# Isomorphism round of a graph network: two batches of edge embeddings in a ring, embedded one to two batches ahead

## The chip, the cores and the metric

The kernel runs on one core of a Trainium2 chip. The metric is the device time of one execution in microseconds (us), lower is better. "Before" is the median of three runs.

## The reference

Four graph networks follow one another on 50,000 nodes of 128 features and 25,000 edges sorted by destination. After each the result is added to its input and layer-normalised. The change touches the second network, the isomorphism round:

```python
edge_emb = edge_attr @ bond_W + bond_b                    # 16 -> 128 per edge
message = gelu(x[src] + edge_emb) * edge_weight1          # exact gelu
agg = segment_sum(message, dst, num_segments=50000)
h = relu(((1 + eps) * x + agg) @ W1 + b1)                 # 128 -> 256
x = layernorm(x + h @ W2 + b2)
```

## The kernel before, in words

The kernel is written with explicit semaphores: every engine has a program of its own, order and waits are written by hand, and instructions of one engine run in program order. Eight rounds of message passing follow one another; round 3 (`k == 3`, kind GIN) is the isomorphism round.

Edges come in 196 tiles of 128, in 28 batches of 7 tiles. Nodes are taken from the top down in 98 halves of 512 nodes, two halves a step, so 49 steps of 1024 nodes. The sum over edges is a matmul of messages with one-hot columns, in two float16 parts: `msg[.., 0:D]` the high part, `msg[.., D:2D]` the low part.

What happens to one batch `e` of edges in round 3:
- GpSimd (POOL, `gin_edges`): seven indirect DMAs fetch the source rows into one of four slots of `raw` (`gather`, L696), one DMA fetches the edge attributes into the single buffer `attr_now` (`attributes`, L709), and `hand_over` waits until both have landed and counts `batch_in` up (L720).
- TensorE (PE, `embed`, L1091): attributes times bond weights, into the two PSUM banks `p_edge` and `p_tr`.
- VectorE (DVE, `embedded_sum`, L1520): rows plus embedding, into `edge_v`, in two parts.
- ScalarE (ACT, `gelu`, L801): gelu of `edge_v` in place.
- POOL (`weigh`, L726): times the edge weight, in place.
- ACT (`batch`, L807): copy to the high part of `msg`.
- DVE (`batch`, L1548): low part, the difference.

There is one `edge_v` and one `embedded` pair of banks. So in the loop over batches `batch(e)` on each engine finishes batch `e` and starts batch `e + 1`: ACT copies `e`, then does the gelu of `e + 1`; DVE makes the low part of `e`, then the sum of `e + 1`; PE embeds `e + 1`.

A step `it` of the round on each engine:
- PE: the batches that step `it + 1` needs; the one-hot matmuls (L1132, L1134) of half 1 of `it` and the residual (L1158); `hidden` of half 0 (L1196); `biased_rows` of half 1 of `it - 1` (L1204, L1208); the one-hot matmuls of half 0 of `it + 1`; `hidden` of half 1; `biased_rows` of half 0 of `it`.
- ACT: the same batches; sums out of PSUM (L847); relu of the hidden layer, half 0 (L856); square root of the variance (L882); sums out of the next half; normalise half (L897); relu, half 1 (L856); normalise the other half.
- DVE (`gin_step`): the same batches; one-hots of half 0 of `it + 1` (L1566); add the residual of half 1 (L1647) and its statistics (L1658, L1663); `scale_rows` (L1775); one-hots of half 1 of `it + 1`; reciprocal and shift for the normalisation (L1672, L1674); add and statistics of half 0.

Which batches belong to a step stands in a list in SBUF that each engine loads into its registers at the head of a step (`values_load`). The list asks for a batch in two of three steps, and for one batch before the first step. The loop over batches is a branch and a loop in registers. ACT loads a function table (`ACT_TABLE_LOAD`) where the next function is not in the loaded one, and at the head of a loop's body or behind it, where the state is not known to the program.

## Time and profile before

| | |
|---|---|
| median of 3 runs | 5383.45 us (5371.6 to 5387.2) |
| profiled execution, its own time | 5378.48 us |
| its span, from the first to the last instruction | 5376.4 us |
| busy share of the span | PE 82%, DVE 64%, ACT 45%, POOL 36% |
| the isomorphism round in the span | first gather at 1484.15 us, steady steps from 1554.5 to 2199.1 us, last batch copied at 2201.47 us |

PE is busy most of the time over the whole kernel. The rounds differ, so the change has to be read in the stretch from 1484 us on, of which the section of rows below shows the part that is used. An idle time with "<-" behind it was ended by the instruction named; "issue" is time in which the engine waited for nothing that the profile shows.

### The profile page before, as it was taken

What the parts mean: (1) busy time and instruction counts of PE and PEld (TensorE: products, weight loads), DVE (VectorE), ACT (ScalarE), POOL (GpSimd) and SP (SyncE); (2) the same over time, 40 slices, a digit from 0 to 9 for tenths busy, and PEclk for the clock granted to TensorE, in tenths of its full rate; (3) what the DMA queues carried; (4) which work ended last, traced back from release to release, by engine and by line L of the source; (5) the groups of instructions that cost most, each with busy time, mean ns of one, the idle gap of its engine ahead of it and who ended that gap; (6) DMA issues with size and microseconds to landing.
All of it is one profiled execution on the core that took longest, in us unless ns stands there. A gap on an engine that the chain in (4) does not pass through costs nothing.

```text
span 5376.4 us, 129953 instructions
## 1 busy us (share of the span) xinstructions
PE 4387.9 (82%) x25128; PEld 2875.8 (53%) x25129; DVE 3446.8 (64%) x10510; ACT 2416.5 (45%) x4969; POOL 1921.9 (36%) x1886
## 2 busy tenths in 40 slices
PE   6998997777878888867777688887799996888895
PEld 4664554433445555535554355543577773677672
DVE  5553454787545555449997688876566663777774
ACT  2442442555257777526664466664222211333332
POOL 5650782654033333016550443310433312333310
PEclk9999999899889999989999899998899999999997
DMA  4663884665234444325553466653444433443432
GB/s 142 217 210 117 260 270 149 195 192 174 90 122 147 149 146 145 111 96 171 174 172 103 145 210 205 211 173 109 137 136 137 140 116 109 129 130 125 128 100 76
DMA packets 443919, 815.61 MB, mean 152 GB/s; under 512 B 70872, under 2 KB 76818, under 8 KB 443828
## 3 DMA queue, kind: packets, MB, share of 16 engines
q1 hardware_dynamic: 389172, 697.28, 38.4%
q0 software_dynamic: 54656, 117.32, 8.9%
q8 instruction: 33, 0.54, 0.0%
q14 instruction: 58, 0.48, 0.0%
HBM read 480.10 MB, written 334.22 MB: 151 GB/s over the span
## 4 chain that ended last, share of the span: by engine, by line
PE 46%; issue 15%; DVE 14%; DVEq 8%; ACT 7%; POOL 5%; DMA 3%; ACTq 2%; SPq 1%; POOLq 0%
PE p_agg L1132 8%; PE p_edge L1119 7%; PE p_agg L1134 7%; PE p_tr L1119 6%; POOL raw L696 4%; PE p_agg L1165 4%; DVE onehot L1566 4%; DVE stats L1658 3%; ACT u L916 2%; PE p_wide L1252 2%; ACT o L897 2%; DVEq L373 2%; PE p_agg L1158 2%; DVEq L1566 2%; PE p_dense L1208 2%
## 5 line engine op out<-in xcount | busy, mean ns | idle before, releaser
L1566 DVE TENSOR_SCALAR onehot<-iota,dst_f,negbase 128x512 f16<-128x512 f16 (+1 forms) x2848 | 1126.1, 449 | 815.6 <-PE p_agg L1165 305.3
L1132 PE MATMUL p_agg<-onehot,msg 128*128 128x512 f16 (+1 forms) x2848 | 1138.3, 400 | 596.5 <-DVE onehot L1566 338.6
L696 POOL DMA_INDIRECT raw<-node_s,src_i x980 | 958.7, 978 | 1449.1 <-DMA node_s<-o 561.4
L1134 PE MATMUL p_agg<-onehot,msg 128*128 128x512 f16 (+1 forms) x2848 | 1140.3, 400 | 0.0
L1132 PEld LDWEIGHTS p_agg<-onehot,msg 128*128 x2848 | 281.8, 99 | 941.4 <-issue 791.1
L696 POOL DMA_INDIRECT raw<-node_x,src_i x392 | 378.8, 966 | 551.0 <-DMA feature<-more_masked 253.6
L897 ACT ACTIVATE o<-v_ring,nmr,rstd 128x128 f32 (+1 forms) x1176 | 472.5, 482 | 76.6 <-DVE nmr L1674 71.5
L1165 PE MATMUL p_agg<-h_in,w 128*128 128x512 f32 x784 | 443.3, 649 | 22.9 <-DMA h_in<-feature 21.9
L1658 DVE BATCH_NORM_STATS2 stats<-v_ring 128x6 f32 (+1 forms) x1960 | 417.7, 278 | 44.3 <-DVE v_ring L1647 15.9
L916 ACT ACTIVATE u<-v_ring,nmr,rstd 128x128 f32 (+1 forms) x784 | 312.5, 481 | 225.0 <-DVE res_in L1704 134.7
L1134 PEld LDWEIGHTS p_agg<-onehot,msg 128*128 x2848 | 282.7, 99 | 219.1 <-issue 32.0
L867 ACT ACTIVATE u<-p_agg,bias 128x512 f32<-128x512 f32 x196 | 134.7, 687 | 551.8 <-PE p_agg L1165 550.8
L1531 DVE SCALAR_TENSOR_TENSOR hid<-type_in,p_wide 128x512 f32<-128x512 f32 (+2 forms) x456 | 261.7, 618 | 89.9 <-PE p_wide L1110 31.7
L752 POOL COPY edge_v<-raw 128x896 f32<-128x896 f32 x56 | 52.2, 931 | 702.6 <-PE p_wide L1110 691.4
L882 ACT ACTIVATE std<-mv,eps_col 128x8 f32<-128x8 f32 x245 | 73.0, 298 | 500.5 <-DVE mv L1663 487.7
L1531 DVE SCALAR_TENSOR_TENSOR more_masked<-type_in,p_wide 128x512 f32<-128x512 f32 (+2 forms) x456 | 267.2, 619 | 39.3 <-PE p_edge L1119 39.3
L1647 DVE TENSOR_TENSOR v_ring<-p_dense,res_in 128x512 f32 (+1 forms) x196 | 135.3, 691 | 205.0 <-PE p_dense L1208 169.1
L1252 PEld LDWEIGHTS p_wide<-w,u 128*128 128x128 f32 x1568 | 205.2, 192 | 101.1 <-issue 89.5
L867 ACT ACTIVATE u<-p_agg,sage_bias 128x512 f32<-128x512 f32 x196 | 133.4, 680 | 269.0 <-PE p_agg L1165 267.3
L1158 PEld LDWEIGHTS p_agg<-hid,h_in 128*128 128x128 f32 x1568 | 224.9, 213 | 47.1 <-issue 38.9
L1158 PE MATMUL p_agg<-hid,h_in 128*128 128x128 f32 x1568 | 233.4, 297 | 0.0
L696 POOL DMA_INDIRECT raw<-in_x,src_i x196 | 194.8, 994 | 105.1 <-issue 54.2
(260 smaller groups left out, 7741.9 us busy)
## 6 DMA issues: line engine op xcount, KB each, us to landing
node_s<-o SPq DMA_DIRECT2D x392, 256.0 KB
h_in<-feature SPq DMA_DIRECT2D x392, 256.0 KB
feature<-u SPq DMA_DIRECT2D x294, 256.0 KB
node_x<-o SPq DMA_DIRECT2D x294, 256.0 KB
res_in<-node_x SPq DMA_DIRECT2D x294, 256.0 KB
h_in<-node_s SPq DMA_DIRECT2D x196, 256.0 KB
h_t<-dinv_scratch SPq DMA_DIRECT2D x196, 256.0 KB
h_in<-in_x SPq DMA_DIRECT2D x98, 256.0 KB
```

The costliest lines, as they stand in the source:

```text
L696: nc.gpsimd.indirect_dma_start(out=raw[:, (e % RING) * BATCH + j, :], out_offset=None, in_=src_d, in_offset=bass.IndirectOffsetOnAxis(ap=s ...
L897: last = nc.scalar.activation(o[:, b, :], tile_ap(v_ring, (it % 2) * BLOCKS + b), ACT.Identity, bias=nmr[0][:, b:b + 1], scale=rstd[0][:, ...
L916: last = nc.scalar.activation(u[:, b, :], tile_ap(v_ring, (it % 2) * BLOCKS + b), ACT.Identity, bias=nmr[0][:, b:b + 1], scale=rstd[0][:, ...
L1119: last = nc.tensor.matmul(related[part][:, j * D:(j + 1) * D], masked[m][:, j * P:(j + 1) * P], w[:, m, :], start=m == 0 and j == 0, stop= ...
L1132: nc.tensor.matmul(p_agg[:, a, :], tile_ap(msg, t, 0, D), oh, start=first, stop=True, skip_group_check=True)
L1134: return nc.tensor.matmul(p_agg[:, a, :], tile_ap(msg, t, D, 2 * D), oh, start=False, stop=True, skip_group_check=True)
L1158: last = nc.tensor.matmul(p_agg[:, a, b * P:(b + 1) * P], h_in[:, 4 * a + b, :], scaled_ident if k == 3 else two_ident, start=False, stop= ...
L1165: nc.tensor.matmul(p_agg[:, a, :], w[:, REL if rel else 3 if k == 1 else 5, :], half_buf(h_in, a), start=False, stop=True, skip_group_chec ...
L1252: last = nc.tensor.matmul(p_wide[:, a, b * D:(b + 1) * D], u[:, 4 * a + b, :], w[:, 2 if k == 0 else 4, :], start=True, stop=True)
L1531: V.scalar_tensor_tensor(out=masked[m][:, cols], in0=flat(type_in[:, bass.ds(e % RING, 1), j0 * P:j1 * P]), scalar=float(m), in1=p_wide[:, ...
L1566: return V.tensor_scalar(tile_ap(onehot, slot), iota[:, :], dst_f[:, bass.ds(t, 1)], negbase[:, bass.ds(it * 2 + a, 1)], ALU.subtract, ALU ...
L1658: last = V.bn_stats(stats[0][:, b, :], tile_ap(v_ring, (it % 2) * BLOCKS + b))
```

## The change

A ring of two batches of float32 edge values, `edge_ring`, takes the place of `edge_v` in this round. It lies in the memory of `type_in`, which only the last two rounds use. Each engine now works on different batches: PE embeds `e + 3`, DVE makes the low part of `e` and the sum of `e + 2`, ACT does the gelu of `e + 1` before the copy of `e`, POOL gathers `e + 4` and hands over `e + 3`.

The batches of a step move too. The list of the step after next is used (`it + 2` in place of `it + 1`). PE does them at the end of its step, behind `biased_rows(it, 0)`; DVE behind the one-hots of half 1 and before `scale_and_move`; ACT behind the relu of half 0 and before `deviation`. Before the first step PE embeds three batches and then the one of the early loop, so four in all, and POOL fetches four batches and hands three over before the first `weigh`. The attribute DMA moves into `hand_over`, behind the gathers of the next batch. The semaphores' totals follow.

```diff
@@ -79,7 +79,7 @@
 
         rows, last, gin, gcn, two = part == 0, part >= 2, part == 3, part >= 4, part == 5
         self.loaded, self.stored = pair("loaded", 16 * NPAIR), pair("put", 16 * NPAIR)
-        self.batch_in = one("taken", 0 if rel else BATCHES + gin)
+        self.batch_in = one("taken", 0 if rel else BATCHES + 3 * gin)
         self.hi_done = one("high", (1 + rel) * BATCHES)
         self.lo_done = one("low", (1 + rel) * BATCHES)
         self.every_ready = one("every", NHALF)
@@ -100,8 +100,8 @@
         self.sum_made = one("sum_made", NHALF, two)
         self.hidden_made = one("hidden_made", 2 * NHALF, gin)
         self.hidden_done = one("hidden_done", 2 * NHALF, gin)
-        self.emb_done = one("emb_done", 2 * BATCHES + 2, gin)
-        self.emb_used = one("emb_used", 2 * BATCHES + 4, gin)
+        self.emb_done = one("emb_done", 2 * (BATCHES + 3), gin)
+        self.emb_used = one("emb_used", 2 * (BATCHES + 2) + 2, gin)
         self.gelu_done = one("gelu_done", BATCHES + 1, gin)
         self.weighed = one("weighed_edges", BATCHES + 1, gin)
         self.res_loaded = pair("residual", 16 * NPAIR, last and part != 4)
@@ -178,6 +178,7 @@
         ew = sb("ew", [P, TILES])
         ew1 = sb("ew1", [P, TILES])
         type_in = sb("type_in", [P, RING, BATCH * P], F16)
+        edge_ring = flat(type_in[:, :, :]).bitcast(F32).rearrange("p (j d) -> p j d", d=D)
         ecol = sb("ecol", [P, TILES, 4], F16)
 
         onehot = sb("onehot", [P, 2 * EVERY + MORE * GROUP, HALF], F16)
@@ -705,16 +706,20 @@
                 all_stored(pool, r - 1)
 
                 def attributes(e):
-                    wait(pool, q.emb_done, 2 * e)
-                    pool.dma_start(attr_now[0:BATCH * DE, :], A["edge_attr_16"][e:e + 1, :, :].rearrange("o f e -> f (o e)")
-                                   ).then_inc(gathered[e % RING], 16)
+                    if 0 < e < BATCHES:
+                        wait(pool, q.emb_done, 2 * e)
+                        pool.dma_start(attr_now[0:BATCH * DE, :],
+                                       A["edge_attr_16"][e:e + 1, :, :].rearrange("o f e -> f (o e)")
+                                       ).then_inc(gathered[e % RING], 16)
 
                 def gather(e):
-                    if e >= RING:
-                        wait(pool, q.emb_used, 2 * (e - RING + 1) + 2)
-                    gather_batch(r, src_d, e)
+                    if e < BATCHES:
+                        if e >= RING:
+                            wait(pool, q.emb_used, 2 * (e - RING + 1) + 2)
+                        gather_batch(r, src_d, e)
 
                 def hand_over(e):
+                    attributes(e)
                     if e < BATCHES:
                         pool.wait_ge(gathered[e % RING], 16 * (per_batch[r] * (e // RING + 1) + landed_before[r]))
                     pool.sem_inc(q.batch_in.semaphore, 1)
@@ -722,21 +727,19 @@
                 def weigh(e):
                     wait(pool, q.gelu_done, e + 1)
                     at = min(e, BATCHES - 1) * BATCH
+                    mine = edge_ring[:, (e % 2) * BATCH:(e % 2 + 1) * BATCH, :]
                     share = ew1[:, at:at + BATCH].unsqueeze(2).to_broadcast([P, BATCH, D])
-                    nc.gpsimd.tensor_tensor(edge_v[:, :, :], edge_v[:, :, :], share, ALU.mult
-                                            ).then_inc(q.weighed.semaphore, 1)
-
-                gather(0)
-                hand_over(0)
-                gather(1)
+                    nc.gpsimd.tensor_tensor(mine, mine, share, ALU.mult).then_inc(q.weighed.semaphore, 1)
+
+                for e in range(3):
+                    gather(e)
+                    hand_over(e)
+                gather(3)
                 for e in range(BATCHES + 1):
                     weigh(e)
-                    if e + 1 < BATCHES:
-                        attributes(e + 1)
-                    if e + 2 < BATCHES:
-                        gather(e + 2)
+                    gather(e + 4)
                     if e < BATCHES:
-                        hand_over(e + 1)
+                        hand_over(e + 3)
 
             def sage(r, src_d, rel, weight):
                 q = S[r]
@@ -796,17 +799,19 @@
             def sage(r, k, rel):
                 q = S[r]
 
+                def edge_slot(e):
+                    return edge_ring[:, bass.ds((e % 2) * BATCH, BATCH), :]
+
                 def gelu(e):
                     wait_apart(act, q.emb_used, 2 * e + 4)
-                    nc.scalar.activation(flat(edge_v[:, :, :]), flat(edge_v[:, :, :]), ACT.Gelu
-                                         ).then_inc(q.gelu_done.semaphore, 1)
+                    nc.scalar.activation(edge_slot(e), edge_slot(e), ACT.Gelu).then_inc(q.gelu_done.semaphore, 1)
 
                 def batch(e):
                     if k == 3:
+                        gelu(e + 1)
                         wait_apart(act, q.weighed, e + 1)
-                        nc.scalar.activation(msg[:, bass.ds(e * BATCH, BATCH), 0:D], edge_v[:, :, :], ACT.Copy
+                        nc.scalar.activation(msg[:, bass.ds(e * BATCH, BATCH), 0:D], edge_slot(e), ACT.Copy
                                              ).then_inc(q.hi_done.semaphore, 1)
-                        gelu(e + 1)
                         return
                     if not rel:
                         wait_apart(act, q.batch_in, e + 1)
@@ -822,7 +827,7 @@
                                          raw[:, bass.ds((e % RING) * BATCH, BATCH), :], ACT.Copy).then_inc(q.hi_done.semaphore, 1)
 
                 def batches(it):
-                    if rel or k == 3:
+                    if rel:
                         if exists(it + 1):
                             each_batch(act, *batch_list(act, PT, it + 1), batch)
                         return
@@ -956,7 +961,8 @@
                     last.then_inc(q.normed2.semaphore, 1)
 
                 def step(it):
-                    batches(it)
+                    if k != 3:
+                        batches(it)
                     if k == 4:
                         relu_out(it - 1, 1)
                         scale_rows(it - 3)
@@ -989,6 +995,7 @@
                     elif k == 3:
                         sums_out(it, 1)
                         hidden(it, 0)
+                        batches(it)
                         deviation(it - 1)
                         sums_out(it + 1, 0)
                         normalise(it - 1, (0,))
@@ -1094,7 +1101,7 @@
 
                 def batch(e):
                     if k == 3:
-                        embed(e + 1)
+                        embed(e + 3)
                         return
                     for part in range(2):
                         wait_apart(pe, q.lo_done, e * 2 + (part - 1))
@@ -1256,10 +1263,9 @@
                     last.then_inc(q.rows_done.semaphore, 1)
 
                 def step(it):
+                    these = ()
                     if exists(it + 1):
-                        if k == 3:
-                            these, (now, after) = odd_list(pe, PT, it * 2 + 1)
-                        elif rel:
+                        if rel or (k == 3 and exists(it + 2)):
                             (e0, e1, e2), (now, after) = later_list(pe, PT, it * 2 + 1)
                             these = e1, e2
                         else:
@@ -1267,17 +1273,22 @@
                     elif exists(it):
                         now = single_list(pe, PT, it * 2 + 1)
                     if k == 3:
-                        if exists(it + 1):
-                            each_batch(pe, *these, batch)
+                        if is_zero(it):
+                            each_batch(pe, e0, e1, batch)
                         if exists(it):
                             first_half(it, 1, now)
                         hidden(it, 0)
                         biased_rows(it - 1, 1)
                         if exists(it + 1):
-                            wait_apart(pe, q.lo_done, these[1])
+                            if these:
+                                wait_apart(pe, q.lo_done, e1)
+                            else:
+                                wait(pe, q.lo_done, BATCHES)
                             first_half(it + 1, 0, after)
                         hidden(it, 1)
                         biased_rows(it, 0)
+                        if these:
+                            each_batch(pe, *these, batch)
                         return
                     if k >= 4:
                         if exists(it):
@@ -1317,7 +1328,8 @@
                         turn_edges(0, part)
                 if k == 3:
                     pe.wait_ge(bond_in, 16 * len(bond_weights))
-                    embed(0)
+                    for e in range(3):
+                        embed(e)
                 end = early_batches(pe, PT, batch if rel or k == 3 else None)
                 wait_apart(pe, q.lo_done, end * (1 + rel))
                 first_half(0, 0, single_list(pe, PT, 0))
@@ -1513,12 +1525,15 @@
             def sage_round(r, k, rel):
                 q, rounds_s = S[r], R[r]
 
+                def edge_slot(e, j0=0, j1=BATCH):
+                    return edge_ring[:, bass.ds((e % 2) * BATCH + j0, j1 - j0), :]
+
                 def embedded_sum(e):
                     wait_apart(dve, q.batch_in, e + 1)
                     for part, (j0, j1) in enumerate(QUARTERS):
                         wait_apart(dve, q.emb_done, 2 * e + (part + 1))
                         V.tensor_tensor(
-                            edge_v[:, j0:j1, :], raw[:, bass.ds((e % RING) * BATCH + j0, j1 - j0), :],
+                            edge_slot(e, j0, j1), raw[:, bass.ds((e % RING) * BATCH + j0, j1 - j0), :],
                             embedded[part][:, 0:(j1 - j0) * D].rearrange("p (j d) -> p j d", d=D), ALU.add
                             ).then_inc(q.emb_used.semaphore, 1)
 
@@ -1545,11 +1560,11 @@
                 def batch(e):
                     if k == 3:
                         wait_apart(dve, q.hi_done, e + 1)
-                        V.tensor_tensor(msg[:, bass.ds(e * BATCH, BATCH), D:2 * D], edge_v[:, :, :],
+                        V.tensor_tensor(msg[:, bass.ds(e * BATCH, BATCH), D:2 * D], edge_slot(e),
                                         msg[:, bass.ds(e * BATCH, BATCH), 0:D], ALU.subtract
                                         ).then_inc(q.lo_done.semaphore, 1)
                         wait_apart(dve, q.lo_done, e + 1)
-                        embedded_sum(e + 1)
+                        embedded_sum(e + 2)
                         return
                     if rel:
                         masks(e, 1)
@@ -1592,10 +1607,9 @@
                         if exists(it):
                             more_onehots(it, 1, single_list(dve, PT, it * 2 + 1))
                         return None, None, None
-                    if rel or k == 3:
+                    if rel:
                         these, (now, after) = odd_list(dve, PT, it * 2 + 1)
-                        if rel:
-                            first_onehots(it + 1, 0, after[0])
+                        first_onehots(it + 1, 0, after[0])
                         each_batch(dve, *these, batch)
                         ahead = None
                     elif exists(it + 2):
@@ -1785,6 +1799,7 @@
                     scale_rows(it - 2)
                     if now:
                         first_onehots(it + 1, 1, after)
+                    batches_ahead(ahead)
                     scale_and_move(it - 1)
                     add(it, 0)
                     statistics(it, 0)
@@ -1840,6 +1855,7 @@
                 first_onehots(0, 1, after[0])
                 if k == 3:
                     embedded_sum(0)
+                    embedded_sum(1)
                 if rel:
                     masks(0, 0)
                 early_batches(dve, PT, batch)
```

## Rows read from the trace of the kernel before

**Rows 1.** The page's chain that ended last: shares of the span by engine.
```profile
PE 46%; issue 15%; DVE 14%; DVEq 8%; ACT 7%; POOL 5%; DMA 3%; ACTq 2%; SPq 1%; POOLq 0%
```

**Rows 2.** Windows of the round: from:to, length; busy us (instructions) of PE, PEld, DVE, ACT, POOL; granted clock; DMA share; GB/s.
```profile
1484.00:1511.00 27.00, 7.30 (x12) 3.16 (x13) 10.41 (x29) 3.18 (x3) 19.62 (x20) 0.50 0.25 69
...
1554.50:2199.10 644.60, 547.44 (x2847) 343.31 (x2848) 353.53 (x1139) 481.15 (x767) 214.74 (x213) 1.00 0.45 146
...
2199.10:2330.00 130.90, 99.90 (x468) 59.18 (x466) 55.75 (x182) 57.64 (x97) 1.77 (x1) 0.91 0.27 90
```

**Rows 3.** Waits, 1554.5 to 2199.1 us: who waited for whom: total us, times, longest.
```profile
PE p_agg L1132 <- DVE onehot L1566: 47.8, 25, 2.4
...
PE p_wide L1196 <- ACT hid L856: 20.3, 23, 0.9
...
DVE msg L1548 <- ACT msg L807: 97.1, 25, 4.4
```

**Rows 4.** Timeline of a step with a batch: start, us, engine, line, operation [idle before].
```profile
1658.16 1.28 ACT L801 ACT_TABLE_LOAD   x1 [3.44 <-DVE edge_v L1520]
...
1659.46 0.95 ACT L801 ACTIVATE edge_v<-edge_v 128x896 f32<-128x896 f32 x1
...
1659.71 0.39 PE L1132 MATMUL p_agg<-onehot,msg 128*128 128x512 f16 x1 [1.89 <-DVE onehot L1566]
...
1660.49 1.68 POOL L726 TENSOR_TENSOR edge_v<-edge_v,ew 128x896 f32<-128x896 f32 x1 [6.68 <-ACT edge_v L801]
...
1661.61 1.65 DVE L1775 TENSOR_TENSOR u<-o,dinv 128x1024 f32<-128x1024 f32 x1
```

**Rows 5.** Timeline of a step without a batch (from 1568.35) and its neighbours.
```profile
1565.14 2.05 PE L1208 MATMUL p_dense<-w,hid 128*128 128x128 f32 x16
...
1568.35 0.39 PE L1132 MATMUL p_agg<-onehot,msg 128*128 128x512 f16 x1 [1.15 <-issue]
...
1572.73 2.05 PE L1208 MATMUL p_dense<-w,hid 128*128 128x128 f32 x16
...
1572.78 1.26 ACT L856 ACTIVATE hid<-p_wide,b_col 128x512 f32<-128x512 f32 x2
...
1577.57 1.23 DVE L1775 TENSOR_TENSOR u<-o,dinv 128x1024 f32<-128x1024 f32 x1
...
1578.72 1.05 DVE L1566 TENSOR_SCALAR onehot<-iota,dst_f,negbase 128x512 f16<-128x512 f16 x3
...
1578.93 2.05 PE L1208 MATMUL p_dense<-w,hid 128*128 128x128 f32 x16
...
1581.91 1.10 PE L1091 MATMUL p_edge<-bond,attr_now 113*128 113x512 f32 x2 [0.93 <-issue]
...
1583.48 0.38 PE L1132 MATMUL p_agg<-onehot,msg 128*128 128x512 f16 x1
...
1587.49 1.09 DVE L1548 TENSOR_TENSOR msg<-edge_v,msg 128x896 f32 x1 [4.41 <-ACT msg L807]
...
1589.91 0.55 DVE L1520 TENSOR_TENSOR edge_v<-raw,p_tr 128x384 f32<-128x384 f32 x1
```

**Rows 6.** Timeline of the start of the round.
```profile
1495.35 0.95 POOL L696 DMA_INDIRECT raw<-node_x,src_i  x1 [2.31 <-DMA raw<-node_x,src_i]
...
1503.84 1.69 POOL L726 TENSOR_TENSOR edge_v<-edge_v,ew 128x896 f32<-128x896 f32 x1
...
1505.46 0.60 POOL L709 DMA_DIRECT2D attr_now<-in_edge_attr  x1
...
1508.11 2.05 PE L1091 MATMUL p_edge<-bond,attr_now 113*128 113x512 f32 x2 [9.95 <-POOLq L720]
```

**Rows 7.** Timeline of PE: first matmul of the steps 42, 43 and 44.
```profile
2199.10 0.38 PE L1132 MATMUL p_agg<-onehot,msg 128*128 128x512 f16 x1
...
2224.02 0.39 PE L1132 MATMUL p_agg<-onehot,msg 128*128 128x512 f16 x1 [1.04 <-issue]
...
2244.53 0.39 PE L1132 MATMUL p_agg<-onehot,msg 128*128 128x512 f16 x1 [1.00 <-issue]
```

## The prediction

> **What bounds the kernel now.** I read the page's chain first: PE has the largest share of it, 46%, and DVE and PE's own issue come next [rows 1]. That is a mean over eight rounds, so I went on to windows of the one round that the change touches. It falls into three parts [rows 2]: a start of 27 us in which PE does next to nothing and its granted clock is 0.50, the lower of its two levels (1.2 GHz); a steady stretch of 644.6 us at a clock of 1.00 (2.4 GHz), in which PE is busy 547 us; and an end without batches. The steady stretch holds the 39 steps from step 3 to step 41. The reader should see there that PE is the bound, but not all the time.
>
> The view of waits says what PE waits for [rows 3]. In 25 steps, those with a batch, it waits 1.9 us for one-hots (47.8 us in all) and in nearly all of them 0.9 us for ACT's relu (20.3 us). Nothing else of size is there. Together that is 68.1 us, and it is what the change can win at most in the stretch. The timeline of such a step shows why [rows 4]: ACT's copy comes late, DVE waits for it (97.1 us in all, [rows 3]), makes low part and sum, and only then starts its one-hots, with which PE starts again; ACT meanwhile waits 3.4 us for the sum before the gelu. The batch stands at the head of the step, in front of everything.
>
> **The change, part by part.** I count a step from its first one-hot matmul, "A". In the step of [rows 5] A is at 1568.35; the first biased rows end at 1574.78 (A + 6.4); `scale_rows` starts at A + 9.2 and takes 1.23; the next one-hots end at 1579.77 (A + 11.4); the second biased rows begin at A + 10.6 and end at A + 12.6. PE's next instruction after those comes 2.98 to 3.21 us after they began [rows 5]: their 1.98 to 2.05 us of matmuls, and some 1 us in which the head of the next step (end of the loop, load of the list's words, register arithmetic) is not yet done.
>
> *Waits removed.* One-hots and relu no longer stand behind the batch: low part, sum, gelu and copy are all of earlier batches, ready when a step begins. All 68.1 us go. What is late next is the question, because the batch still has to pass through DVE and PE inside each step, now at its end.
>
> *The new wait.* PE's embed at the end of the step needs both banks free, so it waits for the sum that DVE makes in the same step. DVE's order until then is add, statistics, `scale_rows`, one-hots, low part, sum. Without disturbance the one-hots end at A + 11.4. From the start of the low part to the end of the second sum it is 1587.49 to 1590.46, 2.97 us [rows 5], so the sums end at A + 14.5 (0.1 us taken for the loop's entry).
>
> One thing disturbs it. ACT does gelu behind the relu of half 0, which ends at A + 5.7 [rows 5]; a table load of 1.28, the gelu of 0.95 and some 0.3 for the list bring it to A + 8.2, and POOL's `weigh` of 1.68 follows at once [rows 4], until A + 10.0. `scale_rows` at A + 9.2 then falls into it, and in such a case it took 1.65 in place of 1.23 and ended 1.1 us after `weigh` [rows 4]: 1661.61 + 1.65 against 1660.49 + 1.68. So it ends at A + 11.1 and not at A + 10.45, and the sums at A + 15.1. The bounds are 14.5 (no overlap) and 15.1. I take 15.1: the overlap follows from ACT's order.
>
> The Trainium skill (SBUF — State Buffer, Who interferes with whom) says that a DVE instruction with two inputs in SBUF and a GpSimd instruction that reads SBUF share a port that the first one keeps to its end. The rows agree, nearly: by the rule `scale_rows` would take its full 1.23 after `weigh`, to A + 11.2, and the whole sum below would be 3 us longer. The same rule speaks for no loss at all if the gelu comes a microsecond later, since `scale_rows` would then be first.
>
> *PE's head after the wait.* Before, the list is loaded and the branches are taken while 2 us of biased rows still run. Now the last thing before the head is a wait for DVE, and PE cannot work ahead past it. Behind it come the two embed matmul pairs, 1.57 us from the first to the next step's A [rows 5], and the head in their shadow. The trace before has no such place. From below: all hidden, about 1.25 us from the last sum to A. From above: the whole 3.2 us that PE needs from the first biased row to its next instruction. The skip of the batch loop, which is in those 3.2, is done before the wait now, so I take 2.6, nearer to the upper row because the head there is seen to outlast 2 us of matmuls.
>
> So a step with a batch is 15.1 + 2.6 = 17.7 us long (15.75 to 18.3). A step without one keeps the old head: 10.6 + 3.1 = 13.7. The 39 steps of the stretch hold 26 of the first kind and 13 of the second: 460.2 + 178.1 = 638.3, against 644.6. The gain there is 6 us of the 68: the wait is mostly changed for another one at the other end of the step.
>
> *Step 42.* It loses its batch to step 41, and the one-hots that it needs beyond the first three tiles no longer stand behind it. It takes 24.9 us, the next one, with as many one-hots and no batch, 20.5 [rows 7]: 4.4 us less. Later steps keep their work. The first batch moves from step 2 to step 1, which I take as even.
>
> *The start.* This part only costs. PE may not begin its first one-hot matmul until it has embedded batch 3, because the early loop's `batch(0)` embeds `e + 3`; before the change it needs batch 1. Embed 3 waits for the fourth hand-over, and POOL reaches that after five gathers, one `weigh` and three attribute loads. Seven gathers take 8.5 us (1495.35 to 1503.84), and from the start of the attribute DMA to the embed it is 2.65 us [rows 6]. With half a microsecond from a hand-over to the next gather: attributes of batch 1 at 1503.85, embed at 1506.5; gathers from 1507.05, attributes at 1515.55, embed at 1518.2; gathers from 1518.75 to 1527.25, `weigh` to 1528.95, gathers from 1529.25 to 1537.75, attributes, embed of batch 3 at 1540.4. Before, the embed that opens the round's steps is at 1508.11 [rows 6]. So everything starts 32.3 us later, and no work of PE covers it: nothing else of the kernel is left to do there. Bounds are 31 and 34 us, since the durations repeat.
>
> *No cost.* The ring and the semaphore totals issue nothing. One table load fewer or more on ACT does not matter: the copy is due at A + 11.4, when DVE begins the low part, and is done by A + 10.4 even with a load of its own. POOL needs per batch about 1.7 + 8.8 + 2.65 + 0.5 = 13.7 us, less than 17.7, so its longer queue (attributes behind the gathers, `weigh` behind the hand-over) is covered; without that cover it would set the step.
>
> **The sum.** 32.3 - 6.3 - 4.4 = +21.6 us on the profiled execution's own 5378.48 us (span 5376.4): 5400 us. That execution is 5 us below the median of the three runs, 5383.45. From that median it would be 5405. A measurement of this kernel tells a change from none at about 0.3%, 16 us.
>
> **The rivals.**
> 1. *The new wait is hidden (faster).* The place is the end of a step with a batch. If PE's head runs in the shadow of the embed and `weigh` misses `scale_rows`, the step is 15.75 us, the stretch 409.5 + 178.1 = 587.6, and the sum 32.3 - 57.0 - 4.4 = -29: 5349 us. It decides from a step of 16.9 us downwards (there the start is paid back); at 16.25 the kernel is 0.3% faster. For it: PE does run ahead through long rows of matmuls. Against it: the idle microsecond behind each row of biased rows.
> 2. *Half of that.* Sums at A + 14.5 and a head of 2.4 give 16.9 us, a stretch of 617.5, and 5379 us: no change.
> 3. *A longer tail.* With a head of 3.2 the step is 18.3, the stretch 653.9, the sum +37: 5416 us. POOL as the bound would show likewise.
> 4. *The start costs nothing.* That needs the first embed not to hold PE; then 5368 us. Against it: PE's order is fixed, and it waits there already [rows 6].
>
> **Chances.** My forecast, 5400 us with 5388 to 5410 around it, 0.42; rival 1 0.18; rival 2 0.24; rival 3 0.11; rival 4 0.05. Rival 1 is faster by over 0.3%, and so is a fifth of rival 4: 0.19. Against the median, the same is 5367 to 5400, but what counts is the ratio, so I put the upper bound at 16 us above the execution's own time, 5395: rival 2, the rest of rival 4 and a quarter of the forecast, 0.38. Slower by over 0.3%: the rest of the forecast and rival 3, 0.43. The range leaves out the outer half of rival 1 and little above: 5358 to 5417 us.
>
> **What would show it.** The waits of PE for one-hots and for the relu should be gone from the stretch, and a wait of PE's embed for the sum should be there in 26 steps, 1.5 to 2.5 us each, with idle time of issue between embed and the next A. Steps with a batch should be 17.7 us apart, steps without 13.7. The first one-hot matmul of the round should come 32 us later than before. `scale_rows` should take about 1.8 in steps with a batch. The prediction is wrong if A follows the last sum within 1.5 us, if `scale_rows` stays at 1.23, or if POOL's start overlaps its hand-overs.

## The result, and the profile after

The changed kernel takes 5403.95 us (median of 6 runs, 5399.29 to 5412.27), the kernel before 5375.88 us in the same comparison (6 runs): a ratio of 1.0052, 95% interval 1.0037 to 1.0066, so slower by half a per cent. The forecast was 5400 us, slower the likeliest of the three. The profiled execution took 5402.63 us, its span is 5400.6.

The windows of the changed kernel answer to [rows 2]: the start, steps 3 to 41 (from first one-hot matmul to first one-hot matmul), and four pieces around one step with a batch.

```profile
1484.00:1545.00 61.00, 16.39 (x28) 6.59 (x29) 12.69 (x33) 4.13 (x4) 41.60 (x43) 0.53 0.20 55
...
1584.50:2226.90 642.40, 556.81 (x2846) 343.94 (x2846) 354.67 (x1141) 403.11 (x703) 227.55 (x195) 0.98 0.45 144
...
1700.00:1710.00 10.00, 7.95 (x52) 5.70 (x50) 6.66 (x20) 5.28 (x7) 5.87 (x4) 1.00 0.59 181
1710.00:1716.00 6.00, 5.10 (x14) 2.52 (x15) 3.23 (x11) 4.34 (x10) 4.54 (x6) 0.62 0.19 49
1716.00:1721.60 5.60, 5.60 (x27) 3.75 (x27) 0.00 (x0) 2.71 (x4) 0.00 (x0) 0.79 0.74 250
1721.60:1728.00 6.40, 6.40 (x37) 4.13 (x36) 5.47 (x18) 4.40 (x6) 4.35 (x3) 1.00 0.24 82
```

The stretch is 2.2 us shorter than before, although PE is busy 9 us longer in it: its granted clock, 1.00 before, is 0.98. The last four rows show one of the six places where it fell: from 1710 on, behind an embed that had waited, the clock is 0.62, then 0.79, and in the last row it is back at 1.00.

The view of waits of the same stretch (engine, line, what it waited for, total us, times, longest) answers to [rows 3].

```profile
PE p_edge L1098 <- DVE type_in L1535: 48.6, 26, 2.3
PE p_agg L1139 <- issue: 33.7, 38, 1.0
PE p_agg L1165 <- DMA h_in<-node_x: 2.4, 6, 0.6
...
DVE v_ring L1661 <- PE p_dense L1215: 173.9, 52, 6.8
```

The waits for one-hots and for the relu, 68.1 us in [rows 3], are gone. In their place the embed waits for the sum in all 26 steps with a batch, 1.87 us each, and 0.9 us of issue stands ahead of the first one-hot matmul. The last row matters later: DVE itself waits long for PE's biased rows, ahead of its add.

The timeline of a step with a batch (A at 1695.28) answers to [rows 4, 5].

```profile
1703.38 1.69 POOL L732 TENSOR_TENSOR type_in<-type_in,ew 128x896 f32<-128x896 f32 x1 [18.91 <-ACT type_in L807]
1704.51 1.63 DVE L1789 TENSOR_TENSOR u<-o,dinv 128x1024 f32<-128x1024 f32 x1
...
1705.87 2.05 PE L1215 MATMUL p_dense<-w,hid 128*128 128x128 f32 x16
1706.06 1.08 DVE L1581 TENSOR_SCALAR onehot<-iota,dst_f,negbase 128x512 f16<-128x512 f16 x3
1707.07 1.07 DVE L1563 TENSOR_TENSOR msg<-type_in,msg  x1
...
1709.73 0.55 DVE L1535 TENSOR_TENSOR type_in<-raw,p_tr 128x384 f32 x1
...
1709.97 1.10 PE L1098 MATMUL p_edge<-bond,attr_now 113*128 113x512 f32 x2 [2.05 <-DVE type_in L1535]
...
1712.71 0.61 PE L1139 MATMUL p_agg<-onehot,msg 128*128 128x512 f16 x1 [0.90 <-issue]
```

`weigh` ends at 1705.07 and `scale_rows`, begun inside it, at 1706.14; one-hots, low part and sum follow until 1710.28, A + 15.0, with one gap, 0.99 us between the low part and the sum, for which DVE waits for its own low part. PE's biased rows were done at 1707.92. From the end of the last sum to the next A it is 2.43 us. PE's load of the next step's list lies in that time (L374, the instructions of that line from 1707 to 1713 us; duration in ns, then start):

```profile
L374 PEldq TENSOR_LOAD <-lists x1: 771/771/771, 1711.2 to 1711.2; - x1
```

The next first matmul takes 0.61 us, not 0.38: this is one of 6 steps of the 39 that begin at the lower clock.

The start answers to [rows 6].

```profile
1506.56 2.04 PE L1098 MATMUL p_edge<-bond,attr_now 113*128 113x512 f32 x2 [8.00 <-POOLq L725]
...
1517.92 2.05 PE L1098 MATMUL p_edge<-bond,attr_now 113*128 113x512 f32 x2 [8.04 <-POOLq L725]
...
1526.89 1.69 POOL L732 TENSOR_TENSOR type_in<-type_in,ew 128x896 f32<-128x896 f32 x1
...
1539.67 2.05 PE L1098 MATMUL p_edge<-bond,attr_now 113*128 113x512 f32 x2 [18.42 <-POOLq L725]
...
1542.79 0.63 PE L1139 MATMUL p_agg<-onehot,msg 128*128 128x512 f16 x1
```

PE waits for each hand-over of POOL, and the embed of batch 3 begins at 1539.67 (forecast 1540.4).

The parts, as differences of the two profiled executions, counted from the round's first gather (0.46 us later here) to the first gather of the next round:

| part | forecast, us | measured, us |
|---|---|---|
| start, to the first one-hot matmul | +32.3 | +31.1 |
| from there to step 3 | 0 | -1.5 |
| steps 3 to 41 | -6.3 | -2.2 |
| steps 42 to 44 | -4.4 | -9.6 |
| rest of the round | 0 | -1.2 |
| round | +21.6 | +16.6 |

The spans differ by 24.2 us, the medians by 28.1. The other 7.6 of the spans lie in rounds that the change does not touch and that came out -3.3 to +5.9 us each in these two executions, so they say nothing of the change.

### The profile page after: what moved, and what is told of

It reads as the page before. It is cut to its first block, busy times and chain, and to the rows that moved or that the text cites. A ratio compares the mean times of both kernels' runs of the same rounds, so it can differ in the third digit from the quotient of the medians.

```text
span 5400.6 us, 130004 instructions
## 1 busy us (share of the span) xinstructions
PE 4388.6 (81%) x25136; PEld 2874.1 (53%) x25137; DVE 3439.7 (64%) x10512; ACT 2324.1 (43%) x4895; POOL 1951.9 (36%) x1886
## 4 chain that ended last, share of the span: by engine, by line
PE 47%; issue 15%; DVE 14%; DVEq 7%; POOL 6%; ACT 5%; DMA 3%; ACTq 2%; SPq 1%; POOLq 0%
PE p_agg L1139 8%; PE p_edge L1126 7%; PE p_agg L1141 7%; PE p_tr L1126 5%; POOL raw L697 5%; PE p_agg L1172 4%; DVE onehot L1581 4%; DVE stats L1672 3%; PE p_dense L1215 2%; ACT u L921 2%; PE p_wide L1203 2%; PE p_wide L1259 2%; PE p_agg L1165 2%; DVE mv L1677 2%; DVEq L1581 2%
## 5 line engine op out<-in xcount | busy, mean ns | idle before, releaser
L697 POOL DMA_INDIRECT raw<-node_x,src_i x392 | 406.5, 1037 | 550.8 <-DMA feature<-more_masked 255.1
L1227 PE MATMUL p_dense<-w,agg_t 128*128 128x128 f32 x1568 | 233.2, 293 | 1.1 <-DVE agg_t L1699 1.1
```

The source lines that it names most:

```text
L697: nc.gpsimd.indirect_dma_start(out=raw[:, (e % RING) * BATCH + j, :], out_offset=None, in_=src_d, in_offset=bass.IndirectOffsetOnAxis(ap=s ...
```

## The experiments

All are edits of the changed kernel, each timed against the kernel before on its chip (medians 5375.95 to 5376.88 us there, as above). "Stretch" is steps 3 to 41; its 26 steps with an embed and 13 without have these mean lengths:

| kernel | stretch, us | with embed | without | time, us | ratio to before (interval) |
|---|---|---|---|---|---|
| changed | 642.4 | 17.70 | 14.01 | 5403.95 | 1.0052 (1.0037 to 1.0066) |
| e1 embed at the head | 618.3 | 16.59 | 14.38 | 5375.78 | 0.9996 (0.9987 to 1.0005) |
| e2 scale_rows last | 604.5 | 16.06 | 14.37 | 5364.77 | 0.9976 (0.9968 to 0.9985) |
| e3 embed in the middle | 611.6 | 16.07 | 14.91 | 5369.04 | 0.9987 (0.9978 to 0.9996) |
| e4 filler | 631.4 | 17.36 | 13.85 | 5394.56 | 1.0040 (1.0025 to 1.0055) |
| e5 start, PE | 637.2 | | | 5395.15 | 1.0043 (1.0029 to 1.0056) |
| e6 start, PE and POOL | 640.2 | | | 5395.97 | 1.0043 (1.0027 to 1.0058) |
| e7 DVE's idle time | 562.5 | 14.40 | 14.48 | 5307.67 | 0.9874 (0.9859 to 0.9889) |
| e8 and the start | 563.9 | 14.42 | 14.53 | 5291.86 | 0.9847 (0.9833 to 0.9860) |

By these intervals the times of e4, e5 and e6 cannot be told from that of the changed kernel. What these three show rests on their traces, of one execution each.

**e1: the embed at the head of the next step.**
```diff
+                        if k == 3:
+                            these, (now, after) = odd_list(pe, PT, it * 2 + 1)
...
+                        if these:
+                            each_batch(pe, *these, batch)
                         if exists(it):
                             first_half(it, 1, now)
...
                         biased_rows(it, 0)
-                        if these:
-                            each_batch(pe, *these, batch)
```


> The changed kernel, but PE takes its embed at the head of the following step, behind the load of its list and before the step's first one-hot matmul. Theory (PE's head was hidden by biased rows and now stands bare behind the wait for the sum): from the start of the embed to the first one-hot matmul it should be about 1.6 us in place of the 2.7 us of the changed kernel's steps with a batch; 26 steps by 1.1 make the stretch of 39 steps about 29 us shorter (613 in place of 642) and the time about 5375 us; the wait for the sum grows or stays, since PE comes to it later but DVE's sum doesn't move. Rival (the microsecond between embed and one-hots belongs to the embed's own loop and waits): the 2.7 us stay, the stretch stays at 640 to 645 and the time at 5400 to 5405.

The timeline of e1 at the start of a step:

```profile
1684.05 1.10 PE L1098 MATMUL p_edge<-bond,attr_now 113*128 113x512 f32 x2 [0.70 <-DVE type_in L1532]
1684.98 0.81 PE L1098 MATMUL p_tr<-bond,attr_now 113*128 113x384 f32 x2
1685.63 0.38 PE L1139 MATMUL p_agg<-onehot,msg 128*128 128x512 f16 x1
```

1.58 us from embed to A, in place of 2.74, with nothing else moved in the program: the head was 1.1 us of each step with a batch, 28 us for the 26, and the time falls by 28. The theory holds, and this alone takes back the whole loss. Two things came out otherwise. The stretch is 24 us shorter where 29 were expected; this execution took 5391.95 us, the slowest of its 11, and its granted clock in the stretch is 0.98. And PE's waits changed:

```profile
PE p_edge L1098 <- DVE type_in L1532: 36.1, 25, 2.3
PE p_agg L1165 <- DMA h_in<-node_x: 19.1, 17, 2.0
```

The wait for the sum is shorter, where it was expected to grow or stay, and one for h_in has come, 19.1 us in place of 2.4.

**e2: scale_rows behind the batch on DVE.**
```diff
-                    scale_rows(it - 2)
                     if now:
                         first_onehots(it + 1, 1, after)
                     batches_ahead(ahead)
+                    scale_rows(it - 2)
```


> The changed kernel, but DVE makes scale_rows behind the batch in place of ahead of the one-hots. Theory (DVE's chain of add, statistics, scale_rows, one-hots, low part and sum sets the length of a step with a batch): the sum comes earlier by the 1.6 us that scale_rows takes, the wait of PE's embed falls from 1.9 us to about 0.3, a step with a batch is about 15.9 us in place of 17.4, and the time falls by 35 to 40 us, to about 5365. First rival (POOL's weigh falls on the one-hots and the low part, and makes these longer by as much as it made scale_rows): half of it, about 5385. Second rival (the embed would have waited anyway, for POOL's attributes): no change, 5400 to 5405, with a wait for the hand-over in place of that for the sum.

The waits of PE in e2's stretch:

```profile
PE p_agg L1139 <- issue: 38.0, 40, 1.1
PE p_agg L1165 <- DMA h_in<-node_x: 14.4, 24, 1.1
PE p_edge L1098 <- DVE type_in L1535: 7.9, 11, 0.9
```

The wait for the sum falls from 48.6 to 7.9 us and the time by 39, as expected. DVE's chain set the step. `scale_rows` takes 1.23 us in all steps here, where `weigh` no longer meets it. The issue rows stay: the head still follows a wait. Some of the 39 us is not the wait itself: the granted clock is 1.00 in this stretch, where six steps of the changed kernel lost 9 us to the lower one, and against that PE waits longer for h_in (14.4 us) and the steps without an embed are 0.36 us longer.

**e3: embed of e + 2 in the middle of the step, start held.**
```diff
-                        embed(e + 3)
+                        embed(e + 2)
...
                             first_half(it, 1, now)
+                        if these:
+                            each_batch(pe, *these, batch)
...
+                if k == 3:
+                    wait_apart(pe, q.batch_in, 4)
```


> The changed kernel, but PE embeds batch e + 2 in the middle of the step, behind its first half, where both banks have been free since the last batch, and not batch e + 3 at the end. The start is held where it was: PE still waits for the fourth hand-over before its first one-hot matmul. Theory: the wait for the sum goes, and the head is hidden by biased rows again. A step with a batch is then set by PE's work, 12.6 us to the end of the biased rows, 1.6 of embed and 1.2 of head, about 15.5 us, or by DVE, which ends its sum at 14.7 us and needs 2.5 more to its next one-hots, about 16.3; with 13.85 for the other steps the stretch is 583 to 604 us in place of 642, and the time 5345 to 5365. The first one-hot matmul stays at 58 us from the round's first gather. Rival (DVE's one-hots come as late as before and PE waits for them in place of the sum): steps stay at 17 us or more, time above 5395.

The waits of PE in e3's stretch:

```profile
PE p_agg L1165 <- DMA h_in<-node_x: 29.0, 23, 2.0
PE p_wide L1203 <- ACT hid L861: 19.0, 23, 1.5
PE p_agg L1139 <- issue: 9.3, 37, 0.5
```

The wait for the sum is gone and the head is covered, but the steps without an embed grew from 14.01 to 14.91 us, and the time missed its 5345 to 5365 by 4 us. PE has waits for h_in (2.4 us in the changed kernel) and for the relu (none there), which neither theory nor rival named. DVE still makes the batch ahead of nmr, behind which ACT's normalise and relu stand, and SP issues the load of h_in behind the stores of what normalise makes; that this order is the cause is read from the code and not tried by itself.

**e4: six matmuls ahead of the embed.**
```diff
+                    if not isinstance(e, int):
+                        for _ in range(6):
+                            nc.tensor.matmul(p_agg[:, 1, 0:P], ident[:, :], ones[:, :], start=True, stop=True,
+                                             skip_group_check=True)
                     wait_apart(pe, q.batch_in, e + 1)
```


> The changed kernel, but in front of each embed at the end of a step PE makes six matmuls of 128x128 f32 into a bank that nobody reads then. They fit in the 1.9 us that the embed waits for the sum (about 0.22 us each). Their results are overwritten and change nothing. Theory (the steps whose matmuls take twice as long, 607 in place of 388 ns, come from PE's idle time before embed and one-hots): no first half of the stretch at a granted clock below 1.00 any more, six slow halves gone, 9 us less, about 5395 us. Rival (the clock falls for another reason, or the fillers come on top of the wait): slow halves stay, or the embed starts later, and the time is 5400 to 5412.

The window of e4's stretch:

```profile
1582.60:2214.10 631.50, 579.97 (x3159) 372.24 (x3159) 352.80 (x1141) 402.73 (x703) 227.58 (x195) 1.00 0.46 147
```

The timeline of PE in one of its steps:

```profile
1705.86 1.50 PE L1097 MATMUL p_agg<-ones,ident 128*128 128x128 f32 x12
1708.08 1.10 PE L1102 MATMUL p_edge<-bond,attr_now 113*128 113x512 f32 x2 [0.72 <-DVE type_in L1539]
...
1710.82 0.39 PE L1143 MATMUL p_agg<-onehot,msg 128*128 128x512 f16 x1 [0.99 <-issue]
```

A clock of 1.00 throughout, no step that begins with a 0.6 us matmul, and a stretch with more work in it that is 11 us shorter. The fillers take 1.5 us of the wait ahead of the embed and leave the idle time ahead of the one-hots as it was (36.7 us of issue in the stretch). So in this kernel the fall of the clock hung on PE's idle time ahead of the embed. The other runs agree: the granted clock of the stretch is 0.98 in e1, e5 and e6, where embeds wait for the sum up to 2.3 or 2.4 us, and 1.00 in e2, where they wait 0.9 at most, and in e3, e7 and e8, where they don't wait. But idle time alone does not decide it: in the kernel before, PE waits up to 2.4 us for one-hots [rows 3] at a clock of 1.00 [rows 2]. Why the clock fell in 6 steps and not in all is open too.

**e5 and e6: the start.** e5 moves PE's embed of batch 3, e6 also POOL's order.
```diff
-                    for e in range(3):
+                    for e in range(2):
                         embed(e)
...
+                        if is_zero(it):
+                            embed(e1 + 2)
                         if these:
                             each_batch(pe, *these, batch)
```
```diff
+                weigh(0)
+                gather(2)
+                hand_over(2)
                 gather(3)
-                for e in range(BATCHES + 1):
+                hand_over(3)
+                gather(4)
+                for e in range(1, BATCHES + 1):
```


> The changed kernel, but the embed of batch 3 comes at the end of step 0 and not before the first one-hot matmul; POOL's order stays. Theory (the start is late because PE waits for the fourth hand-over): from the round's first embed to the first one-hot matmul it is 48 us in the changed kernel and 15 to 16 in the kernel before. Without that wait the next thing is POOL's first weigh, which stands behind four batches of gathers and ends 16 us before the first one-hot matmul; copy, low part and PE's list bring it to about 36 us, so 11 us less, about 5393 us. Rival (the 48 us are given back somewhere else, or the fourth hand-over holds PE at the end of step 0 just as long): the first one-hot matmul moves, but step 3 begins at the same place as in the changed kernel, and the time stays at 5400 to 5405.

> As the run before it, and POOL makes the first weigh behind its second hand-over and the third and fourth hand-over ahead of the gathers that follow. Theory: the first one-hot matmul then waits only for the embed of batch 2, whose attributes land about 24 us after the first embed, so that the first one-hot matmul stands at about 27 us in place of 48; the time is 20 us less than that of the changed kernel, about 5384 us. Rival as before: step 3 begins no earlier than in the changed kernel, 5400 to 5405.

From the first embed to the first one-hot matmul it is 47.6 us in the changed kernel, 37.8 in e5, 28.0 in e6 (16.4 before); to step 3, 89.3, 82.4 and 78.5. So the order of PE did hold the start, but in e6 nearly half of the 19.6 us gained is lost again by step 3. Its timeline, end of step 1:

```profile
1558.79 2.04 PE L1103 MATMUL p_edge<-bond,attr_now 113*128 113x512 f32 x2 [5.72 <-POOLq L725]
1560.62 1.49 PE L1103 MATMUL p_tr<-bond,attr_now 113*128 113x384 f32 x2
...
1561.90 0.63 PE L1144 MATMUL p_agg<-onehot,msg 128*128 128x512 f16 x1
```

PE meets POOL's next hand-over, which stands behind seven more gathers and an attribute load, waits 5.72 us and goes on at the lower clock. So e6 misses its 5384 us by 12, in the direction of its rival, though the rival is not right either: step 3 begins 10.8 us earlier than in the changed kernel. My reading is that a lead of three batches has to be gathered once, at POOL's pace, before or in the first steps; no run changes that pace.

**e7: the batch in DVE's idle time ahead of the add, embed two batches ahead.**
```diff
                         onehots(it + 1, now)
+                    batches_ahead(ahead)
                     add(it - 1, 1)
                     statistics(it - 1, 1)
                     scale_rows(it - 2)
                     if now:
                         first_onehots(it + 1, 1, after)
-                    batches_ahead(ahead)
...
-                        embed(e + 3)
+                        embed(e + 2)
```


> The changed kernel, but DVE makes the low part and the sum in its idle time ahead of the add of the second half, and PE's embed at the end of the step runs two batches ahead in place of three (POOL hands over one batch fewer before the loop). Theory (the sum at the end of DVE's step is the cause of the embed's wait, of PE's bare head and of the slow clock): no wait of the embed for the sum, no first half at a lower clock; a step with a batch is set by PE alone, 15.3 to 16.1 us (16.06 in the run with scale_rows last), the others 13.9, so 578 to 600 us for the 39 steps in place of 642; the first one-hot matmul is at 36 us from the first embed in place of 48 (one batch of gathers fewer). Together about 5345 us, 5325 to 5355. Rival (DVE, later by a batch before its add, makes the next one-hots or nmr too late; PE waits for one-hots, the relu or h_in): steps with a batch stay above 17 us, time 5385 or more.

The window of e7's stretch:

```profile
1575.70:2138.30 562.60, 537.84 (x2847) 336.95 (x2847) 367.84 (x1134) 400.63 (x700) 237.81 (x203) 1.00 0.51 166
```

The waits of PE in it:

```profile
PE p_agg L1139 <- issue: 16.5, 32, 1.0
PE p_agg L1165 <- DMA h_in<-node_x: 9.0, 11, 1.5
```

The timeline of PE at the end of one of its steps:

```profile
1686.15 2.05 PE L1215 MATMUL p_dense<-w,hid 128*128 128x128 f32 x16
...
1688.04 1.02 PE L1098 MATMUL p_edge<-bond,attr_now 113*128 113x512 f32 x2
1688.90 0.81 PE L1098 MATMUL p_tr<-bond,attr_now 113*128 113x384 f32 x2
...
1690.09 0.39 PE L1139 MATMUL p_agg<-onehot,msg 128*128 128x512 f16 x1 [0.38 <-issue]
```

The embed starts as the biased rows end, and nothing waits for the sum. I had expected 15.3 us or more for a step with an embed; it takes 14.40, no longer than one without. From the end of the biased rows to the next A it is 1.67 us with an embed and 0.73 without, means over the stretch, so of the embed's 1.6 us some 0.6 lie where PE's head left it idle anyway. The rest is made up by the steps without an embed, which hold all of the wait for h_in, 9.0 us. PE is busy 96% of the stretch, and the time is 17 us below the range expected. The edit has more parts than its title: DVE uses the list of the next step again, and POOL hands over two batches in place of three ahead of its loop. What DVE's place and the shorter lead are worth singly it does not tell; e3, with the shorter lead and DVE's batch where it was, took 5369.04 us.

**e8: e7 with a start that needs batch 1 alone** (PE embeds batch 2 at the end of step 0, DVE sums it in step 1, POOL's first `weigh` follows its second hand-over).
```diff
-                    for e in range(3):
-                        embed(e)
+                    embed(0)
...
+                        if is_zero(it):
+                            embed(e1 + 1)
...
+                    if isinstance(it, int) and it == 1:
+                        embedded_sum(ahead[0] + 1)
```


> As the run before it, and the start needs batch 1 alone: one embed ahead of the first one-hot matmul besides the early loop's, the embed of batch 2 at the end of step 0, its sum in step 1, and the first weigh of POOL behind its second hand-over. Theory: both costs of the changed kernel are gone; first one-hot matmul at 15 to 17 us from the first embed as in the kernel before, stretch as in the run before it, about 5322 us, 1.0% less than the kernel before. Rival (POOL needs 13 us for each batch anyway and PE meets it in the first steps): the first one-hot matmul moves, but step 3 begins less than 10 us earlier than in the run before it, about 5340 us.

The first one-hot matmul stands at 20.5 us from the first embed (36.3 in e7; 15 to 17 were expected), step 3 at 64.0 (77.4), and the time falls by another 16 us. Here 13.4 of the start's 15.8 us are kept at step 3. That this is because a lead of two needs a batch less from POOL is my reading and not tried by itself. 5291.86 us beats both kernels.

## Why the prediction was right, point by point

*Waits removed.* Right: all 68.1 us of [rows 3] are gone. The working also took them for the most that can be won in the stretch, with nothing else of size there. That was a misreading; the same view of the kernel before has two more rows:

```profile
PE p_edge L1091 <- issue: 18.9, 26, 1.1
PE p_agg L1132 <- issue: 10.2, 16, 1.2
```

e7's stretch is 82 us shorter than that of the kernel before: PE waits 25.5 us in it in place of 97.7, and is busy 537.8 us in place of 547.4.

*The new wait.* Right in place and size. The sum ends at A + 14.7 to 15.3 in the steps that run at the upper clock (forecast 15.1), because `scale_rows` takes 1.33 to 1.93 us behind `weigh` and ends 1.07 us after it. e2, where the two don't meet and the sum no longer waits for `scale_rows`, shows that this chain was the step.

*PE's head after the wait.* Right: 2.4 us from the last sum to A against the 2.6 taken, with the load of the list, 0.77 us, seen in it; e1 covers it and gets 1.1 us per step. Steps at the upper clock are 17.44 us with a batch and 13.83 without (forecast 17.7 and 13.7).

*The clock.* Missing. 26 steps of 17.44 and 13 of 13.83 make 633 us; the stretch took 642. The 9 us between are the six steps at the lower clock, and e4 gives them back. So the stretch would have gained 11 us, gained 2, and the forecast's 6 lies between by two errors that partly cancel: a step with a batch taken 0.26 us too long, and a clock left out.

*Step 42.* Mis-sized: the step takes 16.8 us against 20.5, and steps 42 to 44 together gain 9.6 in place of 4.4. The trace shows where, though no run tests why: in step 42 the granted clock is 1.00 and PE is busy 14.6 us and waits 1.6 for one-hots, while step 43 of the kernel before, on which the 20.5 rest, had a clock of 0.92, 16.3 us of busy PE and a wait of 3.3.

*The start.* Right: 31.1 us for 32.3. The working named PE's order as the cause. e5 and e6 add what it left out: POOL's pace behind it, so that undoing the order returned 7 to 11 us of the 31 by step 3, not all.

*No cost.* Right in the stretch: no wait of PE for a hand-over is left there. e6 shows the price where the cover is missing, 5.72 us.

*Rivals.* The first needed the head in the shadow of other work and `weigh` away from `scale_rows`. Neither happened by itself. e1 covers the head and e2 takes `scale_rows` out of the chain, which is more than to keep `weigh` away from it; the time falls by 28 and 39 us.

*The total.* The closeness of the total is in part luck. The round cost 16.6 us, 5 less than forecast, because all up to step 3 was 2.7 us and all from step 42 on 6.4 us cheaper, and the stretch 4.1 us dearer. The 7.6 us by which the other rounds came out longer, and which nothing here explains, then brought the profiled execution to 5402.63 us.

## What to carry to other kernels

These are lessons of one kernel. Work moved off the head of a step was free only where its last consumer did not stand at the end of the same step: put it where the engine that makes it is idle (here DVE ahead of its add), not merely later. A loop's head was hidden while the engine still had matmuls to run, and stood bare behind a wait, so keep the last wait of an iteration away from its end. Each batch of lead is paid once at the start, at the pace of the slowest feeder: with a lead of three the first one-hot matmul came 47.6 us after the first embed, with two (e7) 36.3.

## What was not expected of the hardware

*The granted clock.* After one of the embed's waits (2.05 us, then 0.90 of issue) it went from 1.00 to 0.62 in a window of 6 us, that is to the lower of its levels (1.2 GHz) for part of it, and a first matmul took 0.61 us in place of 0.38. 1.5 us of matmuls in that wait kept it at 1.00 in all 39 steps of e4. The Trainium skill (TensorE: Matmul & The Clock Gate, HAM oscillation) says that waits between groups of matmuls can bring PE back to its lower clock; in kind these rows agree.

*Who comes first on the port.* The timeline of e7 has a step in which `scale_rows` began 0.01 us ahead of `weigh`:

```profile
1656.34 1.23 DVE L1790 TENSOR_TENSOR u<-o,dinv 128x1024 f32<-128x1024 f32 x1
1656.35 2.76 POOL L732 TENSOR_TENSOR type_in<-type_in,ew 128x896 f32<-128x896 f32 x1 [3.38 <-DMA attr_now<-in_edge_attr]
1657.48 2.42 DVE L1581 TENSOR_SCALAR onehot<-iota,dst_f,negbase 128x512 f16<-128x512 f16 x3
```

Now `scale_rows` keeps its 1.23 us and `weigh` takes 2.76 for 1.68; the one-hots, which start before `weigh` ends, take 2.42 us for 1.05. The Trainium skill (SBUF — State Buffer, Who interferes with whom) says that the first to issue holds the shared port and the other waits. The first two rows agree nearly: had `weigh` waited for the whole of `scale_rows`, it would have taken 2.90 us (estimate: 1.68 and the 1.22 left of `scale_rows`).
